# Second cross attention: the maxima are spread over the partitions by a transposition instead of a float32 product

## The reference, cut to what matters

```python
H, D = (NUM_HEADS, HEAD_DIM)              # 16 heads of 32
q = (x @ Wq.T).reshape(B, N, H, D)        # N = 64 rows of a batch
k = (y @ Wk.T).reshape(B, L, H, D)        # L = 1601 rows of context
v = (y @ Wv.T).reshape(B, L, H, D)
attn = jnp.einsum('bnhd,blhd->bhnl', q, k)
attn = jax.nn.softmax(SCALE * attn, axis=-1)
out = jnp.einsum('bhnl,blhd->bnhd', attn, v).reshape(B, N, C)
return out @ Wp.T + bp
```

## Time and profile before

| | |
|---|---|
| median of 3 runs | 1188.18 us (1187.96 to 1189.69) |
| span of the profiled execution | 1188.1 us |
| time of an execution beside that span | 0.1 us more, median of the runs against the span |
| busy PE, DVE, ACT, POOL | 1145.1, 622.2, 433.4, 332.1 us |
| second cross attention, batches 0 to 6 | about 388 to 1043 us of the span |
| last batch with the self attention | about 1043 to 1114 us, the rest of the self attention and the quantized product to 1188 us |

### The profile page before, as it was taken

How to read it: one execution, slowest core, us unless ns; L and a number is a source line. 1 busy time by engine, 2 the same in 40 slices (tenths; PEclk the granted TensorE clock), 3 DMA queues, 4 the chain that set the end, 5 groups by cost and what they waited for, 6 DMA issues and landing times.

```text
span 1188.1 us, 35228 instructions
## 1 busy us (share of the span) xinstructions
PE 1145.1 (96%) x16186; PEld 866.1 (73%) x16186; DVE 622.2 (52%) x979; ACT 433.4 (36%) x824; POOL 332.1 (28%) x362
## 2 busy tenths in 40 slices
PE   8988999989899999999999999999999999999896
PEld 5533454589688788788888888888888878855673
DVE  2011259555412645645645655655655565576667
ACT  1010152214333434433533533433533543435342
POOL 0000000015000242433334333424433343364512
PEclk9899999999999999999999999999999999999999
DMA  9999980344001101101100200200111110320000
GB/s 369 370 416 410 396 314 30 122 163 160 30 18 59 37 20 60 38 20 61 38 20 24 73 20 24 73 19 24 44 37 37 38 38 20 131 82 2 21 1 36
DMA packets 27620, 115.75 MB, mean 97 GB/s; under 512 B 2504, under 2 KB 3016, under 8 KB 22352
## 3 DMA queue, kind: packets, MB, share of 16 engines
q1 hardware_dynamic: 27472, 113.50, 25.8%
HBM read 112.44 MB, written 1.05 MB: 96 GB/s over the span
## 4 chain that ended last, share of the span: by engine, by line
PE 87%; DVE 6%; DMA 3%; issue 2%; ACT 1%; POOL 0%; SPq 0%; DVEq 0%; ACTq 0%; POOLq 0%
PE SB L431 50%; PE SB L422 7%; PE SC L1202 6%; PE SB L1232 4%; DMA R<-in_ctx_t 3%; PE SB L1268 2%; PE SC L1011 2%; PE SC L1211 2%; PE SC L987 1%; PE SB L987 1%; PE SB L1088 1%; PE SB L1075 1%; PE SC L1194 1%; PE SB L1251 1%; PE SB L415 1%
## 5 line engine op out<-in xcount | busy, mean ns | idle before, releaser
L1716 ACT COPY R<-SB 64x512 f32<-64x512 f32 (+1 forms) x224 | 116.7, 521 | 193.4 <-PE SB L431 191.8
L431 PE MATMUL SB<-high,whigh 128*128 128x512 f32 (+2 forms) x512 | 180.7, 353 | 1.0 <-ACT Z L444 1.0
L1519 DVE TENSOR_REDUCE LN<-SC 128x64 f32<-128x768 f32 x128 | 116.6, 953 | 121.8 <-PE SC L1202 121.8
L431 PE MATMUL SB<-high,wlow 128*128 128x512 f32 (+2 forms) x512 | 178.7, 349 | 0.0
L431 PE MATMUL SB<-low,whigh 128*128 128x512 f32 (+2 forms) x512 | 177.4, 346 | 0.0
L431 PE MATMUL SB<-wlow,high 128*128 128x512 f32 (+1 forms) x416 | 165.8, 399 | 0.0
L431 PE MATMUL SB<-whigh,high 128*128 128x512 f32 (+1 forms) x416 | 164.5, 395 | 0.0
L431 PE MATMUL SB<-whigh,low 128*128 128x512 f32 (+1 forms) x416 | 164.1, 394 | 0.0
L736 POOL TENSOR_TENSOR added<-LN 128x768 f32<-128x768 f32 x32 | 58.8, 1838 | 253.3 <-ACT LN L1748 253.3
L736 POOL TENSOR_TENSOR added<-Z 128x768 f32<-128x768 f32 x32 | 58.6, 1832 | 248.8 <-ACT Z L1748 248.8
L431 PEld LDWEIGHTS SB<-high,whigh 128*128 128x128 f32 x512 | 96.7, 189 | 13.2 <-issue 1.4
(11 more groups left out here) (234 smaller groups left out, 1869.3 us busy)
## 6 DMA issues: line engine op xcount, KB each, us to landing
R<-in_ctx_t SPq DMA_DIRECT2D x32, 1024.0 KB, 6.1
R<-in_ctx SPq DMA_DIRECT2D x8, 3072.0 KB
R<-in_ctx_t SPq DMA_DIRECT2D x16, 644.0 KB, 7.1
R<-in_f SPq DMA_DIRECT2D x4, 2048.0 KB, 15.2
R<-in_f SPq DMA_DIRECT2D x1, 8192.0 KB, 25.4
R<-in_ctx_t SPq DMA_DIRECT2D x12, 512.0 KB, 3.6
R<-in_Wk SPq DMA_DIRECT2D x3, 1024.0 KB, 9.6
R<-in_Wv SPq DMA_DIRECT2D x3, 1024.0 KB, 7.7
```

The costliest lines, as they stand in the source:

```text
L431: last = pe.matmul(out_, lhs[a][:, k, :], rhs[b][:, k, :], start=n == 0, stop=n == 3 * NC - 1)
L1519: inc(dve.tensor_reduce(tops[:, r * T:(r + 1) * T], sc_head[:, :, r, 0:6 * T].rearrange("p g (a q) -> p q g a", q=T), AX.XY, ALU.max), "ha ...
L1716: last = act.copy(keys[nu][64 * half:64 * half + 64, pairs, first * P:first * P + full], src[:, :, 0:full])
```

## The change

Step "b" on PE is written as a transposition of the repeated column instead of a product with the identity. Operands, target and semaphore stay as they were; every value of `spread[u]` is still mx[q] in column q.

```diff
                     elif kind == "b":
                         pe.wait_ge(sem("mx4"), 8 * b + x + 1)
-                        inc(pe.matmul(spread[u], mx[:, x:x + 1].to_broadcast([P, P]), ident[:, :],
-                                      start=True, stop=True), "spread4")
+                        inc(pe.transpose(spread[u], mx[:, x:x + 1].to_broadcast([P, P]), ident[:, :]), "spread4")
                     elif kind == "o":
```

## The result

The median went from 1188.93 us (4 runs of before) to 1182.82 us (4 runs, 1182.54 to 1185.86): ratio 0.9946 [0.9934, 0.9957], 6.1 us less. The forecast was 1179.8 us, within 1178.4 to 1182.2 us, and 8.4 us less. So the direction was right, the gain was 2.3 us smaller than forecast, and the time lies 0.6 us above the range. The base moved as well: the forecast stood on 1188.18 us, the median of three runs, so 0.7 us of the 3.0 us between 1179.8 and 1182.82 us are the base's.

The account below looks back on a forecast made before the run. It took PE's issued instructions to bound the seven batches, and the chain the last batch. Gains of 7.5 us and 0.9 us, together 8.4 us, off 1188.2 us gave 1179.8 us, range 1178.4 to 1182.2 us.

Parts of the forecast that it names:

- The price of a step: PE time saved per step "b": 0.11 us between full products, 0.16 us where the weight load is exposed.
- Rival 1: Load of a repeated column stays at 188 ns, every "b" gives 0.11 us: 6.8 us, 1181.4 us; chance 0.14.
- rival 3: A transposition costs a quarter, 0.055 us instead of 0.11 us: 3.4 us more gain, 1176.4 us; chance 0.04.
- rival 4: A repeated operand is built into the same two passes, so nothing moves: 1188.2 us; chance 0.05.
- rival 2: In part of the pairs PE finds its next input late and half the gain is lost: 1184.0 us; chance 0.05.
- The seven batches: Planned batches where PE is always busy: 27 exposed "b" at 0.16 us and 29 others at 0.11 us, 7.5 us.
- The last batch: Six of its eight "b" lie on the chain, two with hidden and four with exposed loads: 0.9 us.
- the second part: "What the change removes": one transposition replaces two passes with loads on PE; no other queue or wait changes; 8.4 us less.
- Rival 5: Fewer counted products let the clock fall to 0.50 once per batch: 23.8 us lost, 1203.6 us; chance 0.02.

Follow-up runs that it names:

- batches alone: Transposition only in the seven batches, last batch keeping the float32 product: 1184.70 us, 0.9954 of before.
- after on the other chip: The changed kernel, no edit, run on another chip: 1183.30 us, 0.9939 of before at 1190.44 us.
- Before with padding: The kernel before, keeping its float32 product, plus 32 small unread products (128 instructions) near 307 us: 1191.21 us, 1.0014 of before.
- the two changed kernels with padding: The changed kernel plus 32 small unread products, near 240 us (1181.86 us, 0.9928 of before) or near 307 us (1182.17 us, 0.9931).
- the one with the outputs moved: The changed kernel with the last batch's outputs put behind its first projections: 1182.45 us, 0.9934 of before.
- after again: The changed kernel run once more without any edit: 1184.88 us, 0.995 of before at 1189.66 us.
- all three changed kernels with 32 products: The changed kernel with 32 unread products near 240 us (1181.86 us), near 307 us (1182.17 us), and near 307 us with outputs moved (1180.07 us).
- All together: The changed kernel with 32 unread products near 307 us and the last batch's outputs behind its first projections: 1180.07 us, 0.9913 of before.

## Why the prediction was right in direction and too large in size

**The price of a step** was right: 0.111 and 0.162 us for 0.11 and 0.16. Rival 1 fell with loads of 134 ns, rival 3 with the distance of 0.35 us, rival 4 with the 64 records, rival 2 with the absence of any wait of PE on DVE or ACT in the seven batches. The Trainium skill ("TensorE: Matmul & The Clock Gate", section Terms) gives a transpose mode that is four times faster for FP32, and does not say than what; a quarter of the two passes was not seen here: 0.111 us is half of 0.22.

**The seven batches** were forecast at 7.5 us and gave 7.3 to 8.7 us (640.27 to 632.95, 640.95 to 632.29; from the first "b" to the 56th there are 55 steps). The two levels of each kernel, 0.7 us apart, are a spread of executions and none of the change's.

**The last batch** was forecast at 0.9 us, and its own share is 0.9 us by the table. The profiled execution of after lost it all the same, and more.

**The step that failed** stands in the second part: "no queue other than PE's is touched, no DMA is moved and nothing is made to wait that did not wait before". The queue that brings PE's own instructions is touched by every instruction that is taken out. I saw the wait of the earlier trace rows, "issue", that no engine ended, and wrote that PE "should still have no wait there beyond the one of 1.3 us", as if it were a constant. (It lies from 1038.03 to 1039.38 us, among the outputs at the start of the last batch.) It is a fetch that PE outruns, and where it lies, and how many of its kind there are, depends on the count of instructions ahead of it. With the change the first stall is 1.48 to 1.75 us in four runs, where before had 1.35 and 1.17, and a second of 0.8 to 1.4 us comes at line 1202 in three of four (the four are after twice, batches alone, and after on the other chip). Undoing the count by doubling the transposition puts the first back (the 23rd product, 1.03 us); moving the outputs takes it away. The count settles the place of the first stall; that it also makes it longer is not shown. Before with padding has the place moved and 1.09 us, the two changed kernels with padding have the place nearly back and still 1.56 and 1.69 us.

**The clock.** Rival 5 let it fall among the batches; it stayed at 1.00 there, with twice as many transpositions among the products. But it fell to 0.50 (1.2 GHz) in the last batch, where the prediction did not look: behind the stall at line 1202 for 6.8 us in after and 3.4 us in the one with the outputs moved, and behind the first for 3.4 us in after again and in batches alone. In the other nine profiled executions it did not fall between 250 and 1170 us. Among these are all three changed kernels with 32 products, so the transposition alone does not bring it down. What it costs: after takes 76.49 - 74.61 = 1.9 us more behind its last "b", 1.4 us without what belongs to the end of the span (76.49 against 75.06); after again 82.12 - 80.6 = 1.5 us. That the stall makes the clock fall was only argued from their order: in after on the other chip, and in before with padding, there were both stalls and no fall.

**Around the span.** I set the forecast against the median as if an execution took 0.1 us beside its span. It takes 1.67 to 1.77 us in every run of before beside the first experiments, 27 of them, so the profiled execution of 1188.1 us stood near 1189.8 us, the highest of the three runs shown (1189.69). And the packets bear on this too: in before the last packet of instructions starts at 1161.04 us, well within the span, in after at 1185.18 us, behind its end. In the six profiled executions with so late a packet the time beside the span is 1.9 to 2.6 us, in the others 1.7 to 1.8. Before with padding is one of the six, so this needs no transposition. The other three runs of after have 1.8 to 2.3.

So of the 2.3 us that are missing in the median, the runs show three places: longer and additional stalls in the last batch, half clock behind them, and some tenths at the end. How the median divides among them is not settled, since only one of its four runs has a profile; the other three have spans of 1180.6 to 1180.9 us against 1183.4, so they had less of it. All together shows the sum without them: 9.9 us under before. Less before's own stall of 1.2 to 1.4 us, which it lost as well, that is 8.5 to 8.7 us, apart from what its 32 products cost, where 8.4 were forecast. The agreement is not as close as that looks: the interval of the ratio reaches from 8.8 to 11.9 us.

How long a stall is goes in these records with the packet's start. The second stalls of after and of after on the other chip both end 2.67 us after the start of their packet; that packet starts 1.24 us ahead of the stall in the one and 1.89 us in the other, and the stalls are 1.43 and 0.78 us. In after again a packet started 5.1 us ahead of the place of the second stall (1099.86 for 1104.95), and there was none. The packets' own durations vary between 0.9 and 1.4 us. Open is what makes a packet start earlier; no run tried it.

## What to carry to other kernels

Cost a replaced instruction by the distance of starts in both surroundings, hidden and exposed load; here that held to a hundredth of a microsecond. An idle time of PE that the profile gives to "issue", in a dense run of small products, is no constant of the kernel: a change in the number of PE's instructions can move it or make a second one, and its length varied from 0.8 to 1.75 us, so it belongs into the range of the forecast with about one such stall more or less. Where such runs stand, put a few full products between them, and look again after every change of the count.

## What the runs showed of the hardware

**Fetching instructions is not hidden in dense small products.** 104 products with their loads took 1.59 us, so PE would use 256 of them in 256 / 208 x 1.59 = 2.0 us (an estimate); and a packet of 16 KB took 0.9 to 1.4 us to move, and PE went on another 1.3 to 1.6 us later. The stalls were 0.8 to 1.75 us. The Trainium skill ("Runtime: NRT & Kernel Launch", section Instruction fetch mechanics) gives the blocks of 16 KiB and 256 instructions, with which the places of the stalls agree to a single product; it calls the cost of crossing such a boundary mostly hidden, and in these runs it is not.

**A block's end can be followed by count.** 23, 79, 79, 15, 87, 15 and 23 of 104 products came from 0, -112, -112, +16, +128, +16 and 0 instructions ahead of the place, against before.

**The load of a transposition is shorter also for a column repeated 128 times**: 134 ns against 188 ns for a pass of the float32 product with the same operand, and 139 ns for a transposition of a full block.
